# Graph attention and expert network on one core: the scores' broadcast moved into the group's own step, and the gate's running sum moved to VectorE

## The reference, cut to what matters

```python
h = layernorm(x)
Wh = h @ W                                    # 128 graphs, 128 x 256
s1, s2 = Wh @ a1, Wh @ a2                     # two scores per node
e = s1[:, :, None] + s2[:, None, :]
e = where(e > 0, e, 0.2 * e) + log(adj + 1e-6)
x = x + softmax(e, axis=-1) @ Wh              # attention stage
h = layernorm(x)
w = softmax(mean(h, axis=0) @ Wr + br)        # gate: a mean over the graphs
for e in 8 experts:                           # expert stage: three layers each
    y_e = relu(bn(relu(bn(h @ W1[e] + b1[e])) @ W2[e] + b2[e])) @ Wo[e] + bo[e]
x = x + sum over e of w[:, e] * y_e
```

## Time and profile before

| | us |
|---|---|
| median of 3 runs (2492.15 to 2494.12) | 2492.35 |
| the profiled execution | 2494.85 |
| its span, first to last instruction | 2493.1 |
| PE busy | 2409.5 (97%) |
| DVE busy | 1728.2 (69%) |
| ACT busy | 1643.7 (66%) |
| POOL busy | 458.9 (18%) |
| mean granted clock of TensorE | 0.987 |

### The profile page before, as it was taken

How to read it: one execution, slowest core, us unless ns; L and a number is a source line. 1 busy time by engine, 2 the same in 40 slices (tenths; PEclk the granted TensorE clock), 3 DMA queues, 4 the chain that set the end, 5 groups by cost and what they waited for, 6 DMA issues and landing times.

```text
span 2493.1 us, 45081 instructions
## 1 busy us (share of the span) xinstructions
PE 2409.5 (97%) x16304; PEld 2217.6 (89%) x16304; DVE 1728.2 (69%) x2444; ACT 1643.7 (66%) x2497; POOL 458.9 (18%) x487
## 2 busy tenths in 40 slices
PE   7888869999999999999999999999999999999999
PEld 6767658999999999999999999999999999999998
DVE  6888866666666666666666666666666666666665
ACT  6777746666666666666666666666666666666665
POOL 4666632111111100110111111111111100110110
PEclk9999979999999999999999999999999999999999
DMA  5666620000000000000000000000000000000000
GB/s 183 199 189 195 206 89 26 27 26 25 25 25 25 25 25 25 25 17 25 17 17 25 25 25 25 25 25 25 25 25 25 25 25 25 25 17 19 15 17 26
DMA packets 91178, 116.16 MB, mean 47 GB/s; under 512 B 4700, under 2 KB 78856, under 8 KB 91144
## 3 DMA queue, kind: packets, MB, share of 16 engines
q1 hardware_dynamic: 91144, 115.73, 14.4%
HBM read 82.16 MB, written 33.55 MB: 46 GB/s over the span
## 4 chain that ended last, share of the span: by engine, by line
PE 85%; DVE 1%; ACT 0%; issue 0%; ACTq 0%; DVEq 0%
PE ps_y L1186 29%; PE ps_wide L171 29%; PE ps_wide L1168 26%; PE ps_t L132 1%; DVE h_lo L1073 0%; PE ps_y L1234 0%; DVE h L1080 0%; DVE z L1066 0%; ACT h_hi L975 0%; DVE feat_sum L1106 0%; DVE x1t L124 0%; ACT v L980 0%; DVE resb L179 0%; DVE z L1056 0%; DVE h_lo L1088 0%
## 5 line engine op out<-in xcount | busy, mean ns | idle before, releaser
L980 ACT ACTIVATE v<-ps_wide,bn_cols 128x256 f32<-128x256 f32 x768 | 434.7, 566 | 398.6 <-PE ps_wide L1168 271.5
L988 ACT ACTIVATE h<-ps_wide,bn_cols 128x512 f32<-128x512 f32 x512 | 399.2, 780 | 327.2 <-PE ps_wide L171 327.2
L1186 PE MATMUL ps_y<-wo_lo,h_hi 128*128 128x256 f32 x2048 | 578.8, 283 | 0.0
L1186 PE MATMUL ps_y<-wo_hi,h_hi 128*128 128x256 f32 x2048 | 577.2, 282 | 1.6 <-DVE h_lo L1088 1.6
L1186 PE MATMUL ps_y<-wo_hi,h_lo 128*128 128x256 f32 x2048 | 578.3, 282 | 0.0
L1168 PE MATMUL ps_wide<-xq_hi,wq_hi 128*128 128x256 f32 x1792 | 505.6, 282 | 13.8 <-PEq L185 8.4
L1168 PE MATMUL ps_wide<-xq_lo,wq_hi 128*128 128x256 f32 x1792 | 509.2, 284 | 0.0
L1168 PE MATMUL ps_wide<-xq_hi,wq_lo 128*128 128x256 f32 x1792 | 506.5, 283 | 0.0
L1088 DVE TENSOR_TENSOR h_lo<-h,h_hi 128x1024 fp32r<-128x1024 f32 x256 | 318.3, 1243 | 241.9 <-ACT h_hi L994 241.9
L1066 DVE SCALAR_TENSOR_TENSOR z<-ps_wide,bn_cols,v 128x512 f32<-128x512 f32 x256 | 192.2, 751 | 318.2 <-PE ps_wide L1168 318.2
L171 PE MATMUL ps_wide<-h_hi,w_hi 128*128 128x512 f32 x1024 | 404.2, 395 | 2.1 <-DVE h_lo L1073 2.1
(11 more groups left out here) (131 smaller groups left out, 3141.5 us busy)
## 6 DMA issues: line engine op xcount, KB each, us to landing
x_sb<-in_x SPq DMA_DIRECT2D x32, 512.0 KB, 3.5
res<-in_x SPq DMA_DIRECT2D x32, 512.0 KB, 4.5
x1t<-x_scratch SPq DMA_DIRECT2D x32, 512.0 KB, 3.2
resb<-x_scratch SPq DMA_DIRECT2D x32, 512.0 KB, 3.3
out<-resb SPq DMA_DIRECT2D x32, 512.0 KB, 3.0
adj_sb<-in_adj SPq DMA_DIRECT2D x32, 256.0 KB, 4.7
x_scratch<-h SPq DMA_DIRECT2D x16, 512.0 KB, 3.2
x_scratch<-w_bc SPq DMA_DIRECT2D x16, 512.0 KB, 3.1
```

Of the source, the lines that this page charges most:

```text
L980: nc.scalar.activation(v[:, slot, :], ps_l1[:, 0, 0:H], ACT.Identity, bias=bn_cols[:, 1, cols], scale=bn_cols[:, 0, cols]).then_inc(done, 1)
L988: nc.scalar.activation(h2[:, m, :], ps_l2[:, m, :], ACT.Relu, bias=bn_cols[:, 3, cols], scale=bn_cols[:, 2, cols]).then_inc(r2_done, 1)
L1186: mm = nc.tensor.matmul(ps_y[:, b4, :], h[:, c, cols], w[:, e, c, :], start=(e == 0 and k == 0 and b4 % per_bank == 0), stop=(e == E - 1 a ...
```

## The change

Three things are changed, all in the attention stage.

PE makes the scores' broadcast of g at the end of step g, behind h of g-2 and ahead of the transposes of `xn` of g+1. The projection is no longer split: all four graphs come ahead of h. ACT accordingly makes `s_sb` of g in step g. Its order is now: `pT`(g-2), `e_sb`(g-1), `wh`(g), `xn`(g+1), `s_sb`(g), `xnT`(g+1), `mean_all`, the weight copies. Before, it was `pT`(g-2), `s_sb`(g-1), `xn`(g+1), `e_sb`(g-1), the weight copies, `wh`(g), `xnT`(g+1), `mean_all`.

DVE has `l_sb` behind one part of the statistics of x instead of two, and `neg_m` ahead of the third part. It adds all four graphs to `acc`; POOL's two instructions, their tile and their semaphores are gone.

```diff
 (gpsimd)
-                    if exists(t) and not is_step(t, G - 2) and not is_step(t, G - 1):
-                        wait(pool, acc_high_done, num(t))
-                        nc.gpsimd.tensor_tensor(x1s_high[:, :, :], x1[p][:, HB:, :],
-                                                rstd_all[:, num(t), HB:, None].to_broadcast([P, HB, D]),
-                                                ALU.mult).then_inc(x1s_high_done, 1)
-                        pool.wait_ge(x1s_high_done, num(t) + 1)
-                        nc.gpsimd.tensor_tensor(acc[:, HB:, :], acc[:, HB:, :], x1s_high[:, :, :],
-                                                ALU.add).then_inc(acc_high_done, 1)
 (scalar)
                     a = ago(g, 1)
                     if exists(a):
-                        r = a[1]
-                        act.wait_ge(s2b_ready, num(a) + 1)
-                        wait(act, l_done, num(a))
-                        for b4 in range(GB):
-                            last = nc.scalar.activation(s_sb[:, b4, :], ps_s[:, b4, :], ACT.Identity,
-                                                        bias=wh[r][:, b4, D:D + 1])
-                        last.then_inc(s_done, 1)
-                    nxt = ago(g, -1)
-                    if exists(nxt):
-                        normalise(nxt)
-                    if exists(a):
                         act.wait_ge(neg_m_done, num(a) + 1)
                         wait(act, p_done, num(a))
                         for b4 in range(GB):
                             last = nc.scalar.activation(e_sb[:, b4, :], l_sb[:, b4, :], ACT.Exp,
                                                         bias=neg_m[:, b4:b4 + 1])
                         last.then_inc(e_done, 1)
+                    if exists(g):
+                        act.wait_ge(wh_ready, num(g) + 1)
+                        wait(act, h_ready, num(g) - 1)
+                        nc.scalar.activation(wh[p][:, :, :], ps_wide[:, :, 0:D + 2], ACT.Copy).then_inc(wh_copied, 1)
+                    nxt = ago(g, -1)
+                    if exists(nxt):
+                        normalise(nxt)
+                    if exists(g):
+                        act.wait_ge(s2b_ready, num(g) + 1)
+                        wait(act, l_done, num(g))
+                        for b4 in range(GB):
+                            last = nc.scalar.activation(s_sb[:, b4, :], ps_s[:, b4, :], ACT.Identity,
+                                                        bias=wh[p][:, b4, D:D + 1])
+                        last.then_inc(s_done, 1)
...
+                    if exists(nxt):
+                        act.wait_ge(xnT_ready, num(nxt) + 1)
+                        wait(act, wh_ready, num(nxt))
+                        nc.scalar.activation(xnT[:, :, :], ps_xT, ACT.Copy).then_inc(xnT_copied, 1)
...
 (vector)
                         stats_part(0)
-                        stats_part(1)
                         dve.wait_ge(s_done, num(a) + 1)
...
-                        stats_part(2)
+                        stats_part(1)
                         dve.wait_ge(l_done, num(a) + 1)
                         nc.vector.tensor_reduce(neg_m[:, :], l_sb[:, :, :], AX_X, ALU.max,
                                                 negate=True).then_inc(neg_m_done, 1)
+                        stats_part(2)
                         stats_part(3)
...
-                        dve.wait_ge(acc_low_done, num(h) + 1)
+                        dve.wait_ge(acc_step, num(h) + 1)
                         dve.wait_ge(mean2_done, num(h) + 1)
-                        for b4 in range(HB):
+                        for b4 in range(GB):
                             last = nc.vector.scalar_tensor_tensor(out=acc[:, b4, :], in0=x1[h[1]][:, b4, :],
...
-                        wait(dve, x1s_high_done, num(b) - 1)
 (tensor)
-                    if exists(a):
-                        pe.wait_ge(wh_copied, num(a) + 1)
-                        wait(pe, s_done, num(a))
-                        for b4 in range(GB):
-                            last = nc.tensor.matmul(ps_s[:, b4, :], wh[a[1]][:, b4, D + 1:D + 2].to_broadcast([P, P]),
-                                                    ident[:, :], start=True, stop=True)
-                        last.then_inc(s2b_ready, 1)
...
-                        project(g, range(GB // 2))
+                        project(g, range(GB)).then_inc(wh_ready, 1)
                     if exists(b):
...
                         last.then_inc(h_ready, 1)
                     if exists(g):
-                        project(g, range(GB // 2, GB)).then_inc(wh_ready, 1)
+                        pe.wait_ge(wh_copied, num(g) + 1)
+                        wait(pe, s_done, num(g))
+                        for b4 in range(GB):
+                            last = nc.tensor.matmul(ps_s[:, b4, :], wh[g[1]][:, b4, D + 1:D + 2].to_broadcast([P, P]),
+                                                    ident[:, :], start=True, stop=True)
+                        last.then_inc(s2b_ready, 1)
                     if exists(nxt):
                         pe.wait_ge(xn_done, num(nxt) + 1)
```

More of the change, by code:

```diff
@@ L278, in adj_ffn @@
             ve2_done = sem("ve2_done", sa)
-            x1s_high_done = sem("x1s_high_done", sa)
-            acc_low_done = sem("acc_low_done", sa)
-            acc_high_done = sem("acc_high_done", sa)
+            acc_step = sem("acc_step", sa)
             N_SMALL = 2 * 5 + 3
@@ L388, in _ @@
                 nc.gpsimd.memset(minus_one[:, :], -1.0)
-                nc.gpsimd.memset(acc[:, :, :], 0.0).then_inc(acc_low_done, 1)
+                nc.gpsimd.memset(acc[:, :, :], 0.0).then_inc(acc_step, 1)
                 pool.wait_ge(bn_step, 1)
@@ L535, in step @@
                                              ACT.Copy).then_inc(bn_copied, 1)
+                    if exists(nxt):
+                        act.wait_ge(xnT_ready, num(nxt) + 1)
+                        wait(act, wh_ready, num(nxt))
+                        nc.scalar.activation(xnT[:, :, :], ps_xT, ACT.Copy).then_inc(xnT_copied, 1)
+                    t = ago(g, 3)
+                    if exists(t) and not is_step(t, G - 1):
+                        act.wait_ge(stats2_done, num(t) + 1)
+                        nc.scalar.activation(mean_all[:, num(t), :], mv2[t[1]][:, :, 0],
+                                             ACT.Copy).then_inc(mean2_done, 1)
                     if is_step(g, G):
@@ L546, in step @@
                                              w_half[p], ACT.Copy).then_inc(w_hi_done, 1)
[L547 to L559, removed]
                 over_groups(act, step)
@@ L638, in step @@
                                                                   in1=acc[:, b4, :], op0=ALU.mult, op1=ALU.add)
-                        last.then_inc(acc_low_done, 1)
+                        last.then_inc(acc_step, 1)
                     if exists(nxt):
@@ L703, in _ @@
                 last.then_inc(last_stats_done, 1)
-                dve.wait_ge(acc_low_done, G - 1)
-                dve.wait_ge(acc_high_done, G - 2)
+                dve.wait_ge(acc_step, G - 1)
                 dve.wait_ge(rstd2_done, G - 1)
@@ L735, in step @@
                 def step(g, layer):
-                    a = ago(g, 1)
                     b = ago(g, 2)
```

1 line of the change is left out of this document (removed).

## The result

| | before | after |
|---|---|---|
| median of all executions timed, us | 2492.39 (2491.86 to 2494.12, 6) | 2539.31 (2538.52 to 2542.18, 6) |
| profiled execution, us | 2494.85 | 2539.61 |
| its span, us | 2493.1 | 2537.8 |
| mean granted clock | 0.987 | 0.987 |

The changed kernel is slower: ratio 1.0189, 95% interval 1.0176 to 1.0202, which is 46.9 us. The forecast was 2534.0 in a range of 2512 to 2558.

The account below looks back on a forecast made before the run. The prediction took hand-overs between engines in the attention stage, not one engine's work, as the bound. Start 6.8, steps 23.3, locks 4 and low clock 8 gave +42 us, so 2534, in a range of 2512 to 2558.

Parts of the forecast that it names:

- The step chain: Attention steps: loop through projection, h, wh, xn, its transposes and xnT takes 10.71 us a step, +23.3 over 29 steps.
- The start: First attention steps: the load of x delays wh in step 1, so group 2's projection starts 6.8 us later.
- P(1): Start of the projection of group 1, forecast at 27.5 us.
- The lock: First loop: l_sb on DVE stands still beside POOL's wq_lo, making wh 0.5 us late in 8 steps, +4.
- The low clock: Attention steps: PE's clock drops to its low level after idle gaps; ten drops, +8 us.
- The load of x: DVE's step start: waits about 1.4 us for the load, hidden because e ends at 4.9, under 5.42.
- Rival B: Attention steps: the ACT chain is shorter than summed and the load wait sets 10.15 a step; 2515, chance 0.07.
- The sum on DVE: DVE's step: two more acc instructions cost nothing under cover, 0.87 us a step without it.
- the rule taken whole: DVE beside POOL: p_sb could end 1.0 later, passing its cover by about 0.2 a step, 6 us in all.
- A: Attention steps: the low clock comes in every step, costing 29 us instead of 8; 2555, chance 0.12.
- C: Attention steps: the change works as meant and DVE's 9.14 us a step decides; 2481, chance 0.07.

Follow-up runs that it names:

- e3: The changed kernel with xn of g+1 moved on ACT ahead of e_sb of g-1 and the copy of wh: 2499.49 us, ratio 1.0028 to before.
- e8b: e4 with eight idle products on PE between the scores' broadcast and the transposes of xn: 2530.04 us, ratio 1.0150 to before.
- e7: The changed kernel with four idle products on PE between the scores' broadcast and the transposes of xn: 2533.98 us, ratio 1.0159 to before.
- e1: The changed kernel with the running sum shared again, POOL adding two graphs of a group and DVE two: 2536.02 us, ratio 1.0172 to before.
- e9: The changed kernel with xn ahead of e_sb, projection split around h, wh copied in halves, score columns copied apart: 2476.84 us, ratio 0.9932 to before.
- e4: The changed kernel with the score columns copied apart, so scores don't wait for wh: executions of 2610.29, 2607.75, 2541.71 and 2610.60 us.
- e10: e9 with the upper half of the running sum back on POOL: 2472.12 us, ratio 0.9915 to before.

## Why the prediction was right

**The step chain** (forecast 10.71 a step, +23.3). Without drops and locks the steps lie between 10.76 and 10.83: the whole stretch less drops and locks is 313.6, +26.3, or 10.81 a step. The terms that I read from the earlier trace rows held: 0.93 for 0.92, 2.06 for 2.08, 1.02 for 1.02. Three were off by 0.15 or less: projection and h 5.51 to 5.57 instead of 5.42, transposes 1.09 instead of 1.03, hand-over to the projection 0.06 instead of 0.14. e3 shows that this was the mechanism, since putting `xn` out of the loop takes the step to 9.94, and e8b shows that PE's wait ahead of the scores was not part of it.

**The start** (forecast +6.8): +7.5. P(1) came at 27.51, as forecast (27.5). But the projection of that step took 5.44, with a granted clock of 0.69 in 27.5 to 33 us (its row stands below), so PE and not the load set `wh`(1), at 32.98 instead of 32.3.

**The lock** (forecast 8 by 0.5, +4) was sized too high. Timeline of the kernel after, one such step:

```profile
105.32 2.08 POOL L459 TENSOR_TENSOR wq_lo<-w_stage,wq_hi 128x896 f32 x1 [2.27 <-ACT wq_hi L541]
...
106.34 1.61 DVE L597 SCALAR_TENSOR_TENSOR l_sb<-s_sb 128x512 f32<-128x512 f32 x1
...
108.91 1.28 ACT L506 ACTIVATE e_sb<-l_sb,neg_m 128x128 f32<-128x128 f32 x4 [3.36 <-DVE neg_m L602]
...
110.09 1.01 ACT L512 ACTIVATE wh<-ps_wide 128x1032 f32<-128x1032 f32 x1
```

`wq_lo` ends at 107.40 and `l_sb` at 107.95, 0.55 behind it, as I had it. `e_sb` starts 4.73 behind its projection (104.18) instead of 3.75 in the step shown (86.34 less 82.59), 0.98 later. 0.48 of this is slack, and 0.10 goes where `wh` starts ahead of the recorded end of `e_sb` (110.19), so `wh` is 0.40 late where I had 0.5. The step is 11.16 (98.93 to 110.09), 0.33 over the 10.83. Two of the eight coincide with a drop of the clock, where a slow projection hides them, so the sum is 6 by 0.33, +2.0.

**The low clock** (forecast ten drops by 0.8, +8): eight steps of 11.69 to 11.96, each 1.02 longer, +8.2. A little fewer and a little dearer. That the two cancel is luck: no row of the kernel before had such gaps, and the number was taken over from its second loop. Timeline of the kernel after:

```profile
27.51 5.44 PE L716 MATMUL ps_wide<-gw,xnT 128*128 128x258 f32 x16 [1.11 <-ACT xnT L530]
...
68.51 1.74 PE L764 MATMUL ps_th<-ident,xn 128*128 128x128 f32 x8 [0.80 <-ACT xn L489]
...
71.36 4.15 PE L716 MATMUL ps_wide<-gw,xnT 128*128 128x258 f32 x16 [0.26 <-ACT xnT L530]
```

The granted clock was 0.56 in 68.5 to 71 us and 0.87 in 71 to 75.6, and 1.00 in the step shown before (76 to 88). In the lower two rows the transposes take 1.74 instead of 1.09 and the projection 4.15 instead of 3.75: 0.65 and 0.40, together 1.05, and the step is 1.04 over 10.83 (65.46 to 77.33 is 11.87).

**The load of x.** Hidden, as forecast, by 0.48 where I had 0.5 (4.9 against 5.42). The wait itself is larger than the 1.4 that I gave: 79.6 less the first of 12.2 is 67.4 for 31 times, 2.2 each. The load takes 3.87 instead of 3.73, and DVE is ready earlier than I reckoned. In one step of e7 it took 6.20 and was not hidden. The 3.2 us that I estimated from the Trainium skill (DMA: Bandwidth & Descriptors, Anatomy of one DMA) are 0.7 under this row. The section gives its formula for a DMA issued from GpSimd, and this load is issued by SP, so the formula is not for this path. Rival B at 2515 or 2500 did not occur.

**The sum on DVE** (forecast: nothing) cost at most the 3.3 us between the changed kernel and e1. With the cover gone I had put it at 0.87 a step and DVE's own pace at 9.14. e9, with the whole sum on DVE, has steps of 9.05 in most of the first loop, so 9.14 was a little too long; only in the second loop, beside `w_lo`, does the sum show, with 0.66 a step.

**DVE beside POOL.** In the step shown, `p_sb` (79.30) took 0.67 while POOL's `rstd_all` ran from 79.09 to 80.10. The Trainium skill (Advanced Engine Details and Errata, GPSIMD Details) has any DVE instruction with two SBUF inputs conflict with POOL. By this row it does not with a POOL instruction of 128x4; `l_sb` beside `wq_lo` of 128x896 was held (1.61 instead of 0.67). Going by the row was right, the 6 us of the rule taken whole did not come.

**Together.** Forecast 6.8 + 23.3 + 4 + 8 + 0 = 42; found 7.5 + 26.3 + 2.0 + 8.2 - 0.8 + 1.4 = 44.6. The mechanism was right. That the sum is only 2.6 off owes something to luck as well, since the chain was 3.0 too short and the lock 2.0 too long. The 2.2 up to the 46.9 between the medians are the profiled executions: that of before lay 2.5 over its median, that of after 0.3.

**The rivals.** A (half clock in every step) did not occur in this kernel, but e4 shows that it was one merged gap away, and its price was far more than I gave: 2.9 a step instead of 1. C (it works as it is meant) named too weak a condition, that `wh` must not hold up `xn`. e3 meets it and has steps of 9.94, since the scores' wait for `wh` then closes the loop. e9 and e10 take that away too, and are faster than before. My price for C, 2481, lies 4 and 9 us over theirs (2476.84 and 2472.12).

## What to carry to other kernels

A wait that leads the table of waits is not yet one that sets the step: follow each engine's new order by hand from one projection to the next, and add up the loop. An idle stretch of PE is worth only what lies beside it, so the same edit (the score columns copied apart) gave nothing while `xn` was the longer way round, and 0.4 a step once `xn` was out of the loop. Before merging two short gaps of PE into one, look at what follows gaps of that length in the trace.

## What the runs showed of the chip that I had not expected

- **One gap of 2.19 us in each step kept the clock at half for about half of the time, in a stable way.** e4 had every step at 13.65, 0.75 mean granted clock, where the changed kernel with gaps of 1.18 and 0.80 in a step of 10.8 had 0.95 and a drop in about every fourth step. With the gap filled down to 0.41 (e8b) the clock was 1.00. In the profiled execution of e4 the first gap of 2.19 was at once followed by the first projection of 6.63. One execution of four took 2541.71, with a mean granted clock of 0.985 where the other three have 0.955 to 0.957. Why that one kept the clock stays open.
- **Work for nothing made the kernel faster**: four idle products a step (e7), 5 us, with the clock at 1.00 in place of 0.95. But idle work is worth less than a shorter loop: e3, without any, has steps of 9.9 and a granted clock of 1.00 from 31 to 328 us.
- **`l_sb` ends about 0.55 us behind the POOL instruction, wherever in it `l_sb` started.** In the kernel before it starts 0.2 after `wq_lo` and takes 2.47; in the step shown above it starts 1.02 after it and takes 1.61; in e9 it starts 0.40 after `w_lo` and takes 1.42. It needs 0.67 alone, so what is left to do when POOL ends is nearly all of it: DVE did next to nothing of it meanwhile. Such a stop of 0.75 to 0.94 cost 0.66 a step in e9, where DVE had no slack, and 0.33 in the kernel after.
